# Second cross attention: the clamp of the scores moved to VectorE in PSUM, ahead of the maximum

## The reference

```python
attn = jnp.einsum('bhqd,bhkd->bhqk', q, k) * scale      # scale = 16 ** -0.5
attn = jnp.clip(attn, -CLAMP, CLAMP)                    # CLAMP = 10000.0
attn = jax.nn.softmax(attn, axis=-1)
x = jnp.einsum('bhqk,bhkd->bqhd', attn, v).reshape(B, Nq, Cq)
return x @ Wo + bo
```

## Time and profile before

| | us |
|---|---|
| median of 3 runs | 2675.64 |
| lowest and highest run | 2671.07, 2676.82 |
| the profiled execution's own time | 2694.11 |
| its span | 2692.9 |

### The profile page before, as it was taken

The page is one execution under the profiler, slowest core; times in us unless marked ns, Lnnn a source line. Parts: engine busy times, 40 slices in busy tenths (PEclk is TensorE's granted clock), DMA queues, the critical chain, the costliest instruction groups (busy, mean ns, idle before and its releaser), DMA issues.

```text
span 2692.9 us, 66669 instructions
## 1 busy us (share of the span) xinstructions
PE 2484.1 (92%) x26500; PEld 2026.9 (75%) x26500; DVE 1967.9 (73%) x4666; ACT 1667.6 (62%) x4537; POOL 1327.8 (49%) x2117
## 2 busy tenths in 40 slices
PE   6899989898899999998899989999999989999999
PEld 4777767786677777777677777787777868788887
DVE  7778787869687786966565656667766676668998
ACT  4676767676567667765465555656566565666644
POOL 3232334242544434355664664545545464645777
PEclk9899999999899999999999999999999999999999
DMA  6000000000012221000111221100000000000010
GB/s 197 5 26 8 23 9 21 17 18 15 23 54 60 71 58 41 23 25 17 27 50 50 75 78 31 38 28 19 20 17 20 18 21 18 25 6 25 30 38 28
DMA packets 84191, 92.51 MB, mean 34 GB/s; under 512 B 15333, under 2 KB 77289, under 8 KB 83881
## 3 DMA queue, kind: packets, MB, share of 16 engines
q1 hardware_dynamic: 75432, 59.91, 7.2%
q0 software_dynamic: 8448, 28.34, 3.7%
HBM read 65.36 MB, written 22.85 MB: 33 GB/s over the span
## 4 chain that ended last, share of the span: by engine, by line
PE 48%; DVE 24%; POOL 13%; ACT 9%; issue 4%; DMA 2%; another core or an unknown queue 1%; SPq 0%; DVEq 0%; POOLq 0%; ACTq 0%
PE psum L376 12%; PE psum L369 8%; POOL big L1496 6%; PE psum L404 5%; PE psum L453 5%; DVE tiny L796 4%; PE psum L424 3%; PE psum L597 2%; PE psum L469 2%; ACT big L1310 2%; PE psum L383 2%; PE psum L397 2%; DVE big L815 2%; ACT big L1353 2%; PE psum L591 2%
## 5 line engine op out<-in xcount | busy, mean ns | idle before, releaser
L1310 ACT ACTIVATE big<-big 128x512 f32<-128x512 f32 x512 | 313.1, 630 | 211.3 <-DVE big L815 118.5
L796 DVE TENSOR_REDUCE tiny<-psum 128x8 f32<-128x1024 f32 x256 | 311.7, 1219 | 118.3 <-PE psum L453 112.1
L1471 POOL TENSOR_SCALAR tiny<-mv 128x1 f32<-128x1 f32 x224 | 56.9, 254 | 559.1 <-DVE mv L776 556.8
L424 PEld LDWEIGHTS psum<-ident,big 64*128 64x128 f32 x5120 | 208.6, 141 | 137.7 <-ACT big L1310 72.6
L424 PE MATMUL psum<-ident,big 64*128 64x64 f32 x5120 | 254.4, 232 | 62.2 <-ACT big L1310 41.5
L453 PE MATMUL psum<-head_keys,small 64*128 64x256 f32 x2048 | 286.0, 400 | 21.6 <-POOL head_keys L1488 8.0
L1488 POOL TENSOR_TENSOR head_keys<-big,head_rows 128x512 f32<-128x512 f32 x256 | 267.0, 1052 | 0.2
L815 DVE TENSOR_TENSOR big<-psum,tiny 128x512 f32<-128x512 f32 x384 | 251.3, 682 | 3.4
L1519 POOL TENSOR_TENSOR big<-big,tiny 128x512 f32<-128x512 f32 x128 | 135.1, 1061 | 233.6 <-DVE tiny L851 233.1
L1269 ACT ACTIVATE big<-psum 128x512 f32<-128x512 f32 x384 | 213.1, 600 | 59.7 <-PE psum L424 57.5
L1496 POOL TENSOR_SCALAR big<-big 128x512 f32<-128x512 f32 x128 | 190.8, 1503 | 115.2 <-DVE big L812 115.0
(11 more groups left out here) (340 smaller groups left out, 6638.1 us busy)
## 6 DMA issues: line engine op xcount, KB each, us to landing
ctxT<-in_ctxT SPq DMA_DIRECT2D x64, 128.0 KB, 2.2
after_L_xattn<-x SPq DMA_DIRECT2D x64, 128.0 KB, 1.7
mixture_out<-spare SPq DMA_DIRECT2D x46, 128.0 KB
x_in<-in_x SPq DMA_DIRECT2D x32, 128.0 KB
mixture_in<-xn SPq DMA_DIRECT2D x32, 128.0 KB, 1.7
x_in<-after_L_xattn SPq DMA_DIRECT2D x32, 128.0 KB
w_bits<-after_L_xattn SPq DMA_DIRECT2D x32, 128.0 KB, 2.2
spare<-in_L_w SPq DMA_DIRECT2D x2, 1024.0 KB, 6.4
```

The source lines that it names most:

```text
L424: last = pe.transpose(t.ab[:, half, at:at + P // 2], t.e[c][rows, j, :], m.ident[rows, rows])
L796: dve.tensor_reduce(top, s8, AX.X, ALU.max).then_inc(*t.dve.tell(p, f"{l}.top{r}"))
L1310: last = act.activation(flat, flat, ACT.Exp, scale=DH ** -0.5)
```

## The change

In L2, VectorE limits all 1024 scores of a pair in PSUM, in place, on both sides, before it takes the maximum; the small clamp of the eight maxima is dropped; the subtraction becomes the tensor_tensor of the other layers; GpSimd's minimum is dropped with its 128 turns, and ScalarE's exponential waits for the subtraction, as in the other layers. The names of the steps are put in the new order. The strings of `ORDER` are new for all five queues, over all phases; they have as many turns of each lane as before on TensorE, VectorE, ScalarE and SyncE (3624, 3963, 3022 and 341) and 1244 in place of 1372 on GpSimd.

```diff
     if l in SPREAD:
-        dve = dve.replace("top0", "top0 " + SPREAD[l] + "0").replace("top1", "top1 " + SPREAD[l] + "1")
+        dve = dve.replace("top0", SPREAD[l] + "0 top0").replace("top1", SPREAD[l] + "1 top1")
...
-        "pool": NORM["pool"] + " " + NARROW["pool"] + (" below0 below1 below2 below3" if cross == "L2" else "") + " xb",
+        "pool": NORM["pool"] + " " + NARROW["pool"] + " xb",
...
     for r in range(2):
         dve.wait_ge(*t.pe.at(p, f"{l}.s{r}"))
+        if l == "L2":
+            flat = t.ab.rearrange("p r s -> p (r s)")
+            dve.tensor_scalar(flat, flat, CLAMP / DH ** -0.5, -CLAMP / DH ** -0.5, ALU.min, ALU.max
+                              ).then_inc(*t.dve.tell(p, f"{l}.clip{r}"))
+            yield
+            dve.wait_ge(*t.dve.at(p, f"{l}.clip{r}"))
         dve.tensor_reduce(top, s8, AX.X, ALU.max).then_inc(*t.dve.tell(p, f"{l}.top{r}"))
         yield
         dve.wait_ge(*t.dve.at(p, f"{l}.top{r}"))
-        if l == "L2":
-            dve.tensor_scalar(top, top, CLAMP / DH ** -0.5, -CLAMP / DH ** -0.5, ALU.min, ALU.max
-                              ).then_inc(*t.dve.tell(p, f"{l}.clip{r}"))
-            yield
-            dve.wait_ge(*t.dve.at(p, f"{l}.clip{r}"))
...
-            shift = top[:, mine].rearrange("p (h o) -> p h o", o=1).to_broadcast([P, CH, S])
-            if l == "L2":
-                dve.scalar_tensor_tensor(t.e[half], s8[:, mine, :], -CLAMP / DH ** -0.5, shift, ALU.max, ALU.subtract
-                                         ).then_inc(*t.dve.tell(p, f"{l}.e{2 * r + half}"))
-            else:
-                dve.tensor_tensor(t.e[half], s8[:, mine, :], shift, ALU.subtract
-                                  ).then_inc(*t.dve.tell(p, f"{l}.e{2 * r + half}"))
+            dve.tensor_tensor(t.e[half], s8[:, mine, :],
+                              top[:, mine].rearrange("p (h o) -> p h o", o=1).to_broadcast([P, CH, S]), ALU.subtract
+                              ).then_inc(*t.dve.tell(p, f"{l}.e{2 * r + half}"))
...
-                if l == "L2":
-                    act.wait_ge(*t.pool.at(p, f"{l}.below{c}"))
-                else:
-                    act.wait_ge(*t.dve.at(p, f"{l}.e{c}"))
+                act.wait_ge(*t.dve.at(p, f"{l}.e{c}"))
...
-    if l == "L2":
-        for c in range(4):
-            e = t.e[c % 2].rearrange("p h s -> p (h s)")
-            pool.wait_ge(*t.dve.at(p, f"{l}.e{c}"))
-            pool.tensor_scalar(e, e, 0.0, None, ALU.min).then_inc(*t.pool.tell(p, f"{l}.below{c}"))
-            yield
```

More of the change, by code:

```diff
@@ L172 @@
[L172 to L176, removed]
@@ new lines @@
+        "1002133012202231001313010301101201203313321121100120120322302031131313133223002001212221223312312331"
+        "3103333011223012001133221301232130102203232332113131300220200000002330213120330213032030321100221221"
+        "1001330303110121121110021012210202303202030313103223321300112002223312121213233133103303122302112200"
+        "1303200211031332120102120230003110122100023302323320203232101301013312232023010110313002101323331001"
+        "1102121110021023022302030311232121122322332122311213300003122313212233330310123120202331103123321023"
@@ new lines @@
+        "0310101221332311031022312020020233203200103123220313213100310130032121010200133020230132120021012121"
+        "1200111303201203030310132100300113232323121222101201331303101013030330311322100202231122121201032121"
+        "3021020231101133220023030330223323020312012002123011332021221301011331303033120312301203322003301111"
+        "2112001201302302020303311200320032122112223221301230113012101203312310223330311233213022311200210212"
+        "1332313322002110113000000303302232301232012033001312102202330103113013030010123333100211110211200120"
@@ new lines @@
+        "1203223020311332100203102122233223121020120130101322103202203101331233323101031012021010020023302301"
+        "3322112310311032230202032323110011023320311221221033101032231221001102231132001120231320331133120102"
+        "1330222213312221332231232313211212313311333121331220300030032112310023200311210021013301301202133203"
+        "0030030322131112311300030220311201212020323112310010233123132230013122313010110223030322011103131322"
+        "1012012123321332002220112233132230101323010231020132010123312320300013102013313130223032001131322003"
@@ new lines @@
+        "2021103213021021230102021033201202300302230201310301103211230201132131232030211201331301021020233020"
+        "3103122031301122301322011101012321312003201321210033012102223130202331022021332231023123002130100211"
+        "2310013002213121003302230120120123330232011230130123201021323032100110102113032032110011033223200320"
+        "1312320033013013210321220223310302110101332013223011122012313210012023332321330022203131021330202203"
+        "1312312013003013120032132100333322002131331200233021130210232031121332103201010200233000322103203111"
@@ new lines @@
+        "0311220301132110302301213200101013301320221201033223011031022312231001102231232100232013023302201001"
+        "3322233112221330232113013021321010023133300332201021313310022330201120310232311021233010032010213230"
+        "0032210132031131122030211032131232311001013323001202010330312301031301102203133223123230011202112332"
+        "1330021020331032023222201132322102003031002133233200120013332002132303130122310202133210201030002211"
+        "3302132302113031220120130301220323230201211103311230022202233110301122302211301312201213232033210133"
@@ new lines @@
+        "0211122210023031112100331020120201213320321132132030110022310201333312231002120012323300133012031203"
+        "0232112033000300122000332113031022310321012330323230101103312302221103322031103112320322110101021231"
+        "3321321330110211203311120012013312221200313230112023103202113210132313132033002203020332283237287200"
+        "238007383a789007a87330a90378a9078908339783a9038703a307098a09a789a0acb8bc008090b0c87ba7cb8a8cb90c7980"
+        "7a80bc87ab8c9b7a9b80ca80a7ca79b0798ab7a9c00a8ab97c070b0a980a8b98cb65c6b589bac7967c6ca56bc59b5a96b5bc"
@@ new lines @@
+        "1110212323312311033303333303111222203212132322222121101111113331212211030131202230131313331313123121"
+        "1322121002022122021330030302010100310222221020022223232122320303022332331331331001220022000033000003"
+        "1110310021010101110010100010002320010211201113322223131222220022121012011131313131333333323221301112"
+        "1221313300120120111113313100022202222122100202000020203322112321010303233232323322203102323033233233"
+        "1130303313312033320320001200010010133011031121301110100020203110201200003301103013022221122222233312"
@@ L301 @@
+        "31021330300201233320011112023303320011001122232033100012161302237138223300511100a21134232b22143c0303"
+        "2090031410221231432021300013041322403101012342321342001122013324330402101424430301872a3a7b9a887c706a"
+        "9bac8bc9865c599656b5c7a7cb9b566858a79bc65"
     ),
```

208 lines of the change are left out of this document (87 added, 121 removed).

## The result

The changed kernel takes 2611.13 us (median of 3 runs, 2608.25 to 2613.22) against 2675.64: a ratio of 0.9761, 95% interval 0.9745 to 0.9776. I had forecast 2659, with a range of 2634 to 2685. The direction was right; the size was not, by a factor of four: 64.5 us where I had worked out 16.5. The spans of the two profiled executions differ by 86 us, in part because that of before took 2694.11 us, 18 over its median, and one of the four executions of experiment 2's kernel took 10494 us and stays out of its ratio. So I take how much from the medians and from the traces only where.

The account below looks back on a forecast made before the run. The prediction took TensorE as the bound, its idle time in the second phase being what could come back. Gains of 28 and 3.5 us less 15 made 16.5 us: 2659 us from 2675.6, range 2634 to 2685.

Parts of the forecast that it names:

- (g): New order on all five queues: neighbouring turns exchanged, no charge, 8 us either way in the range.
- (a): L2 without GpSimd's minimum: TensorE's 32.0 us of waits for late tiles fall to 4, so 28 us come back.
- (b): GpSimd's other work, such as the masked keys, moves up in its queue: 3.5 us gained, from nothing to 7.3.
- (e): Of the 63 us added to VectorE in the second phase, 15 us lie on the path.
- (c): VectorE's PSUM clamp in L2 takes 1.22 us, 64 times; less the dropped small clamp, VectorE works 63 us longer.
- (d): VectorE's subtraction in L2 as tensor_tensor, 682 ns instead of 685, 128 times: nothing gained.
- (f): A pair's way from scores to last exponential falls from 5.77 to 4.43 us; first tiles come no later.
- Rival 2: TensorE is not the bound; each pair's shorter path counts in full, 86 us, giving 2590 us; chance 0.03.
- Rival 4: Slower: VectorE becomes the gate, TensorE waits for its clamp and maximum, a loss of 10 us, 2686; chance 0.17.

Follow-up runs that it names:

- experiment 2: The kernel before in the new order of turns, with the 128 turns of GpSimd's minimum put back: 2779.5 us, ratio 1.0376 to the kernel before.
- experiment 1: The changed kernel with the old order of turns (GpSimd's without the minimum's 128 turns): 2654.5 us, ratio 0.9925 to the kernel before.
- experiment 5: The changed kernel with the old order up to the second phase and the new order from there on: 2644.4 us, ratio 0.9796 to the kernel before.
- experiment 8: The kernel of experiment 1 with VectorE's new order from the second phase on, where possible without deadlock: 2842.3 us, ratio 1.0531 to the kernel before.
- 9: The kernel of experiment 1 with GpSimd's new order from the second phase on, where possible without deadlock: 2757.3 us, ratio 1.0224 to the kernel before.
- experiment 6: The kernel before, old order, GpSimd doing equally long work nobody reads and ScalarE waiting for the subtraction alone: 2681.0 us, ratio 0.9935 to the kernel before.
- experiment 3: The kernel before, old order, without GpSimd's minimum but with the small clamp of the eight maxima: 2619.9 us, ratio 0.9794 to the kernel before.
- clamp_twice: The changed kernel, new order, with VectorE's clamp done twice in the same turn: 2705.3 us, ratio 1.0027 to the kernel before.

## Why the prediction was wrong

The table in us of 2675, by the ratios:

| | old order | new order |
|---|---|---|
| old code (minimum on GpSimd) | 0 | +101 |
| GpSimd occupied, nobody waits | -17 | +10 (with the clamp) |
| neither minimum nor clamp (old order: the small clamp stays) | -55 | -70 |
| new code (clamp on VectorE) | -20 | -64 |
| new code, clamp twice | not run | +7 |

**Step (g) failed, and it is the one that decided.** I charged nothing for the new order and 8 us either way. With the new code it is worth 44 us (experiment 1), 9 in the first phase and 35 in the second (experiment 5). I had laid the two strings beside each other, found neighbouring turns exchanged, and took small displacements for small effects. Experiments 2, 8 and 9 show how wrong that is: displacements of the same kind cost 101, 162 and 80 us where they don't fit. The pattern of the table, where the new strings gain with the new code and lose with the old code, with idle work or with a second clamp, fits strings that suit one set of step lengths. That is argued from these runs; which displaced turns do it they don't show. Without this step my sum was close, 16.5 us against 20, and that was luck: the terms (a) and (b) together were 23.5 us too small and (e) 20.

**Step (a), the late tiles: right about the wait, too high about its worth.** The wait of the transposes in the matmul rows fell to 1.6 us, under the 4 that I left. But taking the tiles off GpSimd's path gives 17 us (experiment 6), not 28, as long as its queue stays full.

**Step (b), GpSimd's queue: the mis-sized term.** I took 3.5 us; it measured 38 in the old order. I counted only the masked keys, for which TensorE waits directly, and they gave nothing back (7.3 us before, 9.0 without the minimum). I dismissed VectorE's waits for the norms' factors. A late factor makes VectorE's norm late, which TensorE transposes next; by TensorE's direct waits that is 10 of the 38 us, and where the other 28 pass stays open.

**Steps (c) and (d): right.** 1227 ns against my 1.22 us, and the tensor_tensor took 682. The Trainium skill (VectorE: DVE Perf Modes, Why PSUM operands drop a tier) says that an operand in PSUM holds an fp32 operation to its single rate. The trace agrees: the clamp's row is 1227 ns, where twice the 443 ns of the 512 elements on SBUF would make 886.

**Step (e), the clamp on the path: right only for another order.** 15 us forecast; 35 in the old order, 6 in the new one, 71 for a second one. A step has no price of its own in this kernel: VectorE's clamp is priced by the order it stands in. Neither VectorE's share of the chain (24%) nor its direct waits (2%) gave it; of the VectorE time added, 57% reached the end in the old order (35 of 61.5 us: 78.6 of clamp less the 17.1 that experiment 3 spends on the small one), 8% in the new one (6 of 78.6), and 90% of a second clamp (71 of 79).

**Step (f)** held as far as it went: TensorE's whole wait for the exponentials, first and second tiles, is 1.6 us.

**The rivals.** Rival 2's figure (2590) lies nearer to the result than my own, but not by its reason: the paths of the pairs, shortened as in (f), gave only 20 us in the old order. One half of its argument was sound. Weight loads showed 57.7 us of the wait for which the matmul rows showed 34.3, and the matmul rows shrank by 28 us, which I had ruled out ("none of them is touched"). But neither figure was the worth of the late tiles, which experiment 6 puts at 17 us. The Trainium skill (Perfetto Trace Analysis, Identifying the Most-Contended Engine) warns of matmul busy time as a measure of the distance to the limit, and the trace agrees: it moved by 28 us for the same matmuls. Rival 4's mechanism exists: it is the clamp_twice kernel, 7 us slower than before.

What stays open: which turns hide the clamp, since one engine's new string can't be taken alone without harm; how much of each price is a changed granted clock; and what the old code would have gained from strings remade for it. The first phase, whose code is the same, gained 9 us by the order alone, so part of the gain needed no change of the code. Whether the old code could have had more that way wasn't tried.

## What to carry to other kernels

In a kernel whose in-order queues follow a written-out order, price a change together with its order, never apart: the same code was 20 or 64 us faster by the order alone, and the order made for one set of step lengths cost 101 us with another. Count what a full side queue delays at second hand, and not only who waits for it directly: 128 operations that nobody waited for cost 38 us in one order and 74 in the other. Look at the bound engine's weight loads as well as its matmul rows, since overlapping rows can cover a stall, but take neither for the worth of a wait.

## What the runs showed of the hardware

A VectorE tensor_scalar over 1024 fp32 elements in place in PSUM takes 1227 ns, as long as a maximum that writes eight (1219), so writing all of them back to PSUM costs 8 ns more than writing eight results. And the busy time of TensorE's matmul rows is not a constant of the work: the same 26500 matmuls were busy for 2484.1 us before and 2456.1 after, at mean granted clocks of 0.982 and 0.983, and for 2538.9 us in experiment 8, at 0.962.
